# A third place for VectorE in the odd steps: seven subtractions of the row maxima per pair of steps, the fold of the sums in their first round, and the last output written in two halves

## The chip, the cores and the metric

The kernel runs on one core of one Trainium2 chip. The metric is the device time of the program in microseconds (us), the median of several runs. Besides these runs there is one profiled execution, and all rows below are of that one.

## The reference, cut to what matters

```python
def reference(X, Wq, Wk, Wv, Wpost, ffn_weight, ffn_bias):   # X: 4 x 1024 x 128 float32
    xn = layernorm(X)
    Q, K, V = (xn @ W for W in (Wq, Wk, Wv))                 # 16 heads of width 64
    raw = einsum('bshe,bthe->bsth', Q, K / 8)
    attn = softmax(raw, axis=2)
    A = gelu(einsum('bsth,bthe->bshe', attn, V))
    s = xn + A @ Wpost
    xq = mx_quantize(xn)      # blocks of 32: divided by the block's scale, rounded to a 6-bit grid, times the scale
    wq = mx_quantize(ffn_weight)
    g = silu(xq @ wq.T + ffn_bias)
    return X + s * g
```

## The kernel before, in words

The work is a sequence of 64 *steps* `s`. Two consecutive steps are one pair: the even one takes queries 0 to 511 of two heads of one batch, the odd one queries 512 to 1023 of the same heads. A step has four *rounds* `r`, and each round handles two tiles of 128 keys, `j = 2r` and `j = 2r + 1`. Every engine walks through the same double loop over `s` and `r` with its own instruction list, in program order, and semaphores join them.

TensorE's round has this order: `peak`, the raw scores of a *later* step (product of the rounded parts alone, two matmuls into the two banks of `peaks`), whose only purpose is the maximum of each row; `score` for tile 2r; `score` for tile 2r + 1; a second `peak`; then `weigh` for the two tiles of the round before, the product of probabilities and values into `acc`. Each `score` is three pairs of matmuls of split operands (L530), the two halves of the array working side by side, and a fourth pair (L537) that adds minus the row maxima out of `max_rows`. Where a next head has to be projected, the second `score` of a round is written mixed with that projection (L436), and the second peak's two matmuls are among it. Value projections (L448) and small transposes stand in some rounds too. `peaks` exists once: `peak_ready` lets no new peak start until VectorE has reduced the one before. `scores` exists twice: a tile may be written when the tile two before it has been read.

VectorE's round has the reduction of the first peak (`reduce_peaks`, L1066), then for the tiles listed in `BY_VECTOR` the subtraction of the maxima out of `scores` into `probs` (`subtract_maxima`, L1099), then the reduction of the second peak, and smaller work. For a tile that VectorE subtracts, TensorE leaves out the fourth pair. Before, these are tiles 0, 2, 4 and 6 in even steps and tile 0 in odd ones; the last step (63) follows the even list. `maxima` of the next step are joined and transposed in round 1 (`join_maxima`, `turn_squares`) and spread through DRAM into `max_rows` and `max_rep`. In the odd steps VectorE also quantises one tile of 128 rows for the gate: part 0 at the end of round 1, part 1 in round 2 just ahead of the second reduction, part 2 at the end of round 2, part 3 at the head of round 3 (`quantise_tile`, L1018 to L1029). Three odd steps, one ahead of each new batch, have one more operation there, `low_x` (L1052).

ScalarE takes the exponentials (L787), in the order that `order(s)` gives: in a round whose even tile goes to VectorE, the odd tile first. GpSimd (POOL) adds the eight probability tiles of a step into `prob_sum`, seven additions (L937), and multiplies the outputs of the step two before by the inverse sums (`normalise`, L893). `fold_sums` (L1104) on VectorE folds a finished `prob_sum` and waits for the seventh addition; `invert_sums` follows after a trip through DRAM. The fold of step s - 1 stands in round 3 of each step, in step 63 in round 1.

In step 0 no maxima are ahead yet: each round has three peaks, of which ScalarE copies the first into `att[0]` (`copy_peaks`), from where `reduce_copied` (L1059) reduces it. The start before that has eight first peaks, with `warm` matmuls between them (L605).

After step 63 TensorE runs `post` (L661), the output projection, chunk by chunk: eight chunks `c` of four tiles of 128 rows. Chunks 0 and 1 are run together head by head, then 2, 3 and so on. A chunk's bank of `scores` is used again two batches later: chunk 4 waits until chunk 0 has been read (`post_read`). VectorE's `result` adds xn (L1209), multiplies by the gate (L1212) and adds the input (L1215), and SyncE (SP) stores the chunk.

## Time and profile before

| | |
|---|---|
| median of 3 runs | 1353.72 us (1353.44 to 1354.28) |
| the profiled execution, its own time | 1353.71 us |
| its span | 1351.9 us |
| TensorE (PE) busy | 1332.1 us, 99% |
| GpSimd (POOL) busy | 1177.3 us, 87% |
| VectorE (DVE) busy | 1117.5 us, 83% |
| ScalarE (ACT) busy | 764.4 us, 57% |
| one pair of steps, 547.30 to 586.32 | 20.11 us + 18.91 us |
| chain that ended last | PE 91%, POOL 2%, DVE 2%, DMA 2%, ACT 1% |

The profiled execution's own time lies 1.8 us above its span: what lies ahead of the first and behind the last recorded event. The granted clock of TensorE is 1.00 (the level of 2.4 GHz) in nearly every stretch. A busy share is a mean over the span; a matmul's recorded duration overlaps the next one's, so the distance between starts is what a matmul costs. On VectorE too an instruction begins before the one ahead has ended: a reduction is recorded with 1.23 us, and the next instruction starts 1.14 us after it. Lines such as L516 are those of the kernel before.

### The profile page before, as it was taken

Reading aid. Unit: us, or ns where it says so; the run is one execution under the profiler, and the core shown is the slowest. Engines: PE = TensorE matmul, PEld = TensorE weight load, DVE = VectorE, ACT = ScalarE, POOL = GpSimd, SP = SyncE. Lnnn points to the kernel's source line nnn. Section 1 sums busy time; section 2 is a strip of 40 time slices with the busy share of each in tenths; the row PEclk is TensorE's granted clock in tenths of the full one; section 3 lists DMA queues with packets and bytes.
Section 4 is the critical chain, followed back from the end, with each engine's and each line's share of the span. In section 5 each row is a group of like instructions: output and inputs, shape, how many; then the busy total and the mean of one; then the engine's idle time right before and its main releaser. Section 6 shows DMA issues by size and latency. Waiting matters only on the chain.

```text
span 1351.9 us, 27029 instructions
## 1 busy us (share of the span) xinstructions
PE 1332.1 (99%) x10076; PEld 777.9 (58%) x10076; DVE 1117.5 (83%) x1509; ACT 764.4 (57%) x1072; POOL 1177.3 (87%) x551
## 2 busy tenths in 40 slices
PE   7999999999999999999999999999999999999998
PEld 4555555555555555555555555555555555555488
DVE  7689888888888888888888889888888888888623
ACT  4555665555556566555556566555555655555583
POOL 3689999998999999998999999999899999999940
PEclk9999999999999999999999999999999999999999
DMA  2011212211221212211122121212112111211484
GB/s 84 17 50 58 65 43 81 58 47 53 65 60 48 66 58 59 64 58 50 58 66 57 43 66 58 63 45 66 56 43 58 49 41 37 66 50 32 154 269 149
DMA packets 110636, 88.20 MB, mean 65 GB/s; under 512 B 70446, under 2 KB 84526, under 8 KB 110508
## 3 DMA queue, kind: packets, MB, share of 16 engines
q1 hardware_dynamic: 110508, 86.48, 21.6%
q8 instruction: 82, 1.34, 0.4%
q14 instruction: 46, 0.38, 0.1%
HBM read 70.19 MB, written 16.25 MB: 64 GB/s over the span
## 4 chain that ended last, share of the span: by engine, by line
PE 91%; POOL 2%; DVE 2%; DMA 2%; ACT 1%; issue 1%; SPq 0%; POOLq 0%; DVEq 0%
PE acc L588 33%; PE scores L530 24%; PE peaks L516 13%; PE extra L436 8%; PE scores L537 6%; PE extra L448 4%; POOL prob_sum L937 2%; PE scores L661 2%; PE extra L477 1%; DVE half_maxes L1066 1%; DMA sum_scratch<-group_sums 1%; ACT probs L787 1%; PE extra L484 0%; PE extra L459 0%; DMA probs<-att_scratch 0%
## 5 line engine op out<-in xcount | busy, mean ns | idle before, releaser
L937 POOL TENSOR_TENSOR prob_sum<-prob_sum,probs 128x1024 f32<-128x1024 f32 x384 | 917.5, 2389 | 79.8 <-ACT probs L787 34.5
L1066 DVE TENSOR_REDUCE half_maxes<-peaks 128x2 f32<-128x1024 f32 x500 | 612.2, 1224 | 150.1 <-PE peaks L516 143.9
L787 ACT ACTIVATE probs<-scores 128x1024 f32<-128x1024 f32 x353 | 355.4, 1025 | 473.4 <-PE scores L537 473.4
L588 PE MATMUL acc<-probs,vals 128*64 128x512 f32 x2048 | 492.5, 601 | 0.0
L516 PE MATMUL peaks<-k_hi,q_hi 64*128 64x512 f32 x1008 | 277.6, 451 | 6.5 <-DVE half_maxes L1066 4.7
L530 PE MATMUL scores<-q_hi,k_hi 64*128 64x512 f32 x1024 | 251.6, 393 | 1.1 <-DVE probs L1099 1.1
L530 PE MATMUL scores<-q_hi,k_lo 64*128 64x512 f32 x1024 | 250.0, 390 | 0.0
L530 PE MATMUL scores<-q_lo,k_hi 64*128 64x512 f32 x1024 | 249.0, 389 | 0.0
L588 PEld LDWEIGHTS acc<-probs,vals 128*64 128x64 f32 x2048 | 128.0, 136 | 210.1 <-issue 201.7
L516 PEld LDWEIGHTS peaks<-k_hi,q_hi 64*128 64x128 f32 x1008 | 116.6, 183 | 195.1 <-DVE half_maxes L1066 116.8
L1099 DVE TENSOR_TENSOR probs<-scores,max_rep 128x1024 f32<-128x1024 f32 x159 | 193.1, 1214 | 7.1 <-PE scores L530 5.7
L537 PE MATMUL scores<-max_rows,minus_r 64*128 64x512 f32 x690 | 182.1, 389 | 0.0
L937 POOL TENSOR_TENSOR prob_sum<-probs 128x1024 f32<-128x1024 f32 x64 | 153.6, 2399 | 23.7 <-ACT probs L787 23.7
L787 ACT ACTIVATE probs<-probs 128x1024 f32<-128x1024 f32 x159 | 170.0, 1069 | 1.9 <-DVE probs L1099 1.9
L530 PEld LDWEIGHTS scores<-q_lo,k_hi 64*128 64x128 f32 x1024 | 118.9, 185 | 22.0
L530 PEld LDWEIGHTS scores<-q_hi,k_lo 64*128 64x128 f32 x1024 | 118.9, 184 | 18.2
L530 PEld LDWEIGHTS scores<-q_hi,k_hi 64*128 64x128 f32 x1024 | 118.9, 185 | 15.8 <-issue 3.4
L893 POOL TENSOR_TENSOR att<-raw,inv_sum 128x512 f32<-128x512 f32 x64 | 98.2, 1534 | 20.5 <-DMA inv_sum<-inv_scratch 20.5
L537 PEld LDWEIGHTS scores<-max_rows,minus_r 64*128 64x128 f32 x690 | 86.8, 184 | 12.9
L1104 DVE TRANSPOSE_TENSOR_REDUCE group_sums<-prob_sum 128x32 f32<-128x1024 f32 x64 | 79.0, 1234 | 6.4 <-POOL prob_sum L937 6.4
L448 PEld LDWEIGHTS extra<-w_v,xTs 128*64 128x64 f32 x1024 | 57.3, 137 | 28.1 <-issue 27.0
L448 PE MATMUL extra<-w_v,xTs 128*64 128x128 f32 x1024 | 69.1, 276 | 0.2 <-DVE q_lo L1046 0.2
(170 smaller groups left out, 1223.7 us busy)
## 6 DMA issues: line engine op xcount, KB each, us to landing
max_rep<-max_scratch SPq DMA_DIRECT2D x63, 512.0 KB, 4.0
inv_sum<-inv_scratch SPq DMA_DIRECT2D x128, 128.0 KB, 2.9
att_scratch<-att SPq DMA_DIRECT2D x48, 256.0 KB, 2.3
probs<-att_scratch SPq DMA_DIRECT2D x8, 512.0 KB, 5.5
max_scratch<-turned SPq DMA_DIRECT2D x252, 1.0 KB
split_back<-att_scratch SPq DMA_DIRECT2D x6, 512.0 KB, 5.6
sums<-sum_scratch SPq DMA_DIRECT2D x128, 8.0 KB, 2.1
out_dram<-xn SPq DMA_DIRECT2D x8, 256.0 KB, 3.7
```

Source lines behind the costliest of these rows:

```text
L436: return mm(extra[:, :], left[own[h], at:at + P], right[own[h], halves[half]], start=(h == 0 and i == 0), stop=(h == 1 and i == 2), tile_p ...
L448: last = mm(w[own[h], t * P:(t + 1) * P], xT[:, tokens:tokens + DH], w_v[:, at:at + P], start=True, stop=True, tile_position=col[h])
L516: return mm(peaks[:, h, :], q_hi[z][own[h], t * P:(t + 1) * P], k_hi[z][own[h], keys], start=True, stop=True, tile_position=row[h])
L530: return mm(w[:, h, :], left[z][own[h], ks], right[z][own[h], qs], start=(i == 0), stop=(i == 2 and by_vector(s, j)), tile_position=row[h])
L537: return mm(w[:, h, :], sign[own[h], :], rows[own[h], :], start=False, stop=True, tile_position=row[h])
L588: last = mm(acc[own[h], :], vals[(s // 2) % 2][:, j, own[h]], probs[j][:, h, :], start=(k == 0), stop=(k == KT - 1), tile_position=col[h])
L787: sa.activation(probs[j][:, :, :], src[:, :, :], ACT.Exp, scale=DH ** -0.5).then_inc(probs_ready, 1)
L893: gp.tensor_tensor(by_32(att[p % HP][:, halves[s % 2]]), by_32(raw[s % 2][:, :]), inv[s % 2][:, :].rearrange("p (i b) -> p b i", i=SQ), AL ...
L937: gp.tensor_tensor(prob_sum[s % 2][:, :, :], before[:, :, :], probs[order(s)[j]][:, :, :], ALU.add).then_inc(probs_summed, 1)
L1066: v.tensor_reduce(half_maxes[:, :, f // 2, f % 2], peaks[:, :, :], AX.X, ALU.max).then_inc(peaks_read, 1)
L1099: v.tensor_tensor(probs[j][:, :, :], scores[j % 2][:, :, :], max_rep[s % 2][:, :, :], ALU.subtract).then_inc(subtracted, 1)
L1104: v.tensor_reduce(group_sums[:, :], prob_sum[s % 2][:, :, :].rearrange("p h (b i) -> p (h b) i", i=SQ), AX.X, ALU.add, apply_transpose=Tru ...
```

## The change

It has eight parts. (1) `BY_VECTOR` of the odd steps goes from tile 0 to tiles 0, 4 and 6. (2) The fold that stood in round 3 of the odd steps goes to their first round; in step 63 it goes from round 1 to round 0. (3) In step 0 the copied peak is reduced after the second peak rather than ahead of it. (4) `warm` has one matmul rather than two. (5) ScalarE runs one exponential on a spare value ahead of the first copies. (6) GpSimd gets, behind its last `normalise`, a multiplication and an addition for each of the eight chunks: rows xn times gate, plus the input. (7) `result` on VectorE has two operations in place of three, the product of the projection and the gate and one addition, and waits for GpSimd's. (8) The last chunk is projected, combined and stored in two halves, the second one through `acc`.

```diff
@@ -92,7 +92,7 @@
-    BY_VECTOR = ((0, 2, 4, 6), (0,))
+    BY_VECTOR = ((0, 2, 4, 6), (0, 4, 6))
     def by_vector(s, j):
         return s > 0 and j in BY_VECTOR[s % 2 if s < NS - 1 else 0]
...
@@ -180,6 +180,9 @@
         x_back = [rows_back[0][:, :], rows_back[1][:, :], k_lo_back[1][:, 0:HALF], k_lo_back[1][:, HALF:S], raw[0][:, :], inv[0][:, :], raw[1][:, :], inv[1][:, :]]
         TC = HALF // P
         NC = NT // TC
+
+        pieces = [(c, 0, TC) for c in range(NC - 1)] + [(NC - 1, 0, TC // 2), (NC - 1, TC // 2, TC // 2)]
+        lies_in = lambda c, t0: acc[:, :] if t0 > 0 else scores[c // 2 % 2][:, c % 2, :]
         scores = [ctx.enter_context(nc.psum_tensor(f"scores{u}", [P, 2, HALF], F32)) for u in (0, 1)]
         acc = ctx.enter_context(nc.psum_tensor("acc", [P, HALF], F32))
...
@@ -393,10 +396,10 @@
             sp.wait_ge(normalised, NS)
             for c in range(4, NC):
                 load_x_back(c)
-            for c in range(NC):
-                sp.wait_ge(result_done, c + 1)
-                sp.dma_start(out_t[:, c * TC:(c + 1) * TC, :], xn[c // 2][:, c % 2 * TC:(c % 2 + 1) * TC, :]).then_inc(written, 16)
-            sp.wait_ge(written, 16 * NC)
+            for i, (c, t0, nt) in enumerate(pieces):
+                sp.wait_ge(result_done, i + 1)
+                sp.dma_start(out_t[:, c * TC + t0:c * TC + t0 + nt, :], xn[c // 2][:, c % 2 * TC + t0:c % 2 * TC + t0 + nt, :]).then_inc(written, 16)
+            sp.wait_ge(written, 16 * len(pieces))
         @block.tensor
         def _(pe):
...
@@ -601,8 +604,7 @@
             def warm():
-                for _ in range(2):
-                    mm(acc[:, :], ones_r[:, :], max_rows[0][:, :], start=True, stop=True)
+                mm(acc[:, :], ones_r[:, :], max_rows[0][:, :], start=True, stop=True)
             pe.wait_ge(consts_set, N_SET)
...
@@ -653,13 +655,14 @@
             weigh(NS - 1, 6)
             weigh(NS - 1, 7)
-            def post(p, half):
+            def post(p, half, t0=0, nt=TC):
                 b, h = p // HP, p % HP
-                for t in range(TC):
+                w = lies_in(2 * b + half, t0)
+                for t in range(t0, t0 + nt):
                     for i in (0, 1):
                         tokens = half * HALF + t * P + i * DH
-                        last = mm(scores[b % 2][own[i], half, t * D:(t + 1) * D], home[p][:, tokens:tokens + DH], wp[:, h, :],
-                                  start=(h == 0 and t == 0), stop=(h == HP - 1 and t == TC - 1), tile_position=col[i])
+                        last = mm(w[own[i], (t - t0) * D:(t - t0 + 1) * D], home[p][:, tokens:tokens + DH], wp[:, h, :],
+                                  start=(h == 0 and t == t0), stop=(h == HP - 1 and t == t0 + nt - 1), tile_position=col[i])
                 if h == HP - 1:
                     last.then_inc(post_done, 1)
...
@@ -672,9 +675,12 @@
             for b in range(1, B):
                 for half in (0, 1):
                     above(pe, post_read, 2 * b + half - 3)
-                    for p in range(b * HP, (b + 1) * HP):
-                        pe.wait_ge(gelu_done, p + 1)
-                        post(p, half)
+                    if (b, half) == (B - 1, 1):
+                        pe.wait_ge(acc_read, NS)
+                    for t0, nt in [(t0, nt) for c, t0, nt in pieces if c == 2 * b + half]:
+                        for p in range(b * HP, (b + 1) * HP):
+                            pe.wait_ge(gelu_done, p + 1)
+                            post(p, half, t0, nt)
         @block.scalar
         def _(act):
...
@@ -793,6 +799,8 @@
             for p in (0, 1):
                 square(p)
                 root(p)
+
+            sa.activation(spare[:, :], eps[:, :], ACT.Exp)
             for half in (0, 1):
                 copy_xT(("x", 0, half))
                 for name in "qk":
...
@@ -940,6 +948,14 @@
             normalise(NS - 2)
             normalise(NS - 1)
+            for c in range(NC):
+                rows = xn[c // 2][:, c % 2 * TC:(c % 2 + 1) * TC, :]
+                pool.wait_ge(gated, c // 2 + 1)
+                gp.tensor_tensor(rows, rows, gate[:, c * TC:(c + 1) * TC, :], ALU.mult).then_inc(gated_rows, 1)
+                pool.wait_ge(gated_rows, c + 1)
+                pool.wait_ge(x_loaded_back[c], 16)
+                gp.tensor_tensor(rows, rows, x_back[c].rearrange("p (t d) -> p t d", d=D), ALU.add).then_inc(rest_ready, 1)
+
         @block.vector
         def _(dve):
             v = nc.vector
...
@@ -1146,9 +1162,7 @@
                     if half == 1 and r == 3:
                         quantise_tile(n, 3)
                     for at in todo[:1]:
-                        if s == 0:
-                            reduce_copied(r, *at)
-                        else:
+                        if s > 0:
                             reduce_peaks(*at)
                     if by_vector(s, 2 * r):
                         subtract_maxima(s, 2 * r)
...
@@ -1156,10 +1170,10 @@
                         gate_argument(n - 1)
                     if half == 1 and r == 2:
                         quantise_tile(n, 1)
-                    if half == 1 and r == 3 and s < NS - 1:
-                        fold_sums(s - 1)
                     for at in todo[1:2]:
                         reduce_peaks(*at)
+                    if s == 0:
+                        reduce_copied(r, *todo[0])
                     if r == (1 if s > 0 else 2) and s + 1 < NS:
                         join_maxima(s + 1)
                     if r == 1 and s > 1 and (half == 1 or False or s == NS - 2):
...
@@ -1181,7 +1195,7 @@
                         quantise_tile(n, 2 * r - 2)
                     if half == 1 and r == 2 and turns_x:
                         low_x(("x", later, 0))
-                    if s > 0 and half == 0 and r == 3 or s == NS - 1 and r == 1:
+                    if s > 0 and (half, r) in ((0, 3), (1, 0)):
                         fold_sums(s - 1)
                     if r == 3 and s == NS - 1:
                         invert_sums(NS - 2)
...
@@ -1201,26 +1215,23 @@
                         if half == 0 and r == 3 and n % HP == 5:
                             block_inverse(later)
-            def result(c):
+            def result(i):
+                c, t0, nt = pieces[i]
                 b, half = c // 2, c % 2
-                rows = xn[b][:, half * TC:(half + 1) * TC, :]
-                as_rows = lambda a: a.rearrange("p (t d) -> p t d", d=D)
-                dve.wait_ge(post_done, c + 1)
-                v.tensor_tensor(rows, as_rows(scores[b % 2][:, half, :]), rows, ALU.add).then_inc(post_read, 1)
-                dve.wait_ge(post_read, c + 1)
-                dve.wait_ge(gated, b + 1)
-                v.tensor_tensor(rows, rows, gate[:, c * TC:(c + 1) * TC, :], ALU.mult).then_inc(res_step, 1)
-                dve.wait_ge(res_step, c + 1)
-                dve.wait_ge(x_loaded_back[c], 16)
-                v.tensor_tensor(rows, rows, as_rows(x_back[c]), ALU.add).then_inc(result_done, 1)
+                ts = slice(half * TC + t0, half * TC + t0 + nt)
+                gates = gate[:, b * NB + half * TC + t0:b * NB + half * TC + t0 + nt, :]
+                dve.wait_ge(post_done, i + 1)
+                dve.wait_ge(gated_rows, c + 1)
+                v.tensor_tensor(gates, lies_in(c, t0)[:, 0:nt * D].rearrange("p (t d) -> p t d", d=D), gates, ALU.mult).then_inc(post_read, 1)
+                dve.wait_ge(post_read, i + 1)
+                dve.wait_ge(rest_ready, c + 1)
+                v.tensor_tensor(xn[b][:, ts, :], xn[b][:, ts, :], gates, ALU.add).then_inc(result_done, 1)
             gate_argument(NP - 1)
             fold_sums(NS - 1)
             invert_sums(NS - 1)
-            for c in (0, 1):
-                result(c)
-            for c in range(2, NC):
-                result(c)
+            for i in range(len(pieces)):
+                result(i)
 _INS = ["L0_attn_X", "L0_attn_Wq", "L0_attn_Wk", "L0_attn_Wv", "L0_attn_Wpost", "L0_ffn_weight", "L0_ffn_bias"]
```

The list of VectorE's instructions in an odd step, rounds 1 (its end) to 3. First the kernel before: the three L1018 to L1020 are part 0 of the quantisation, L1066 is the reduction of a peak, L1104 the fold.

```order
L1018 TENSOR_TENSOR extra<-extra,small 128x128
L1019 TENSOR_SCALAR quant_tmp<-extra 128x128
L1020 SCALAR_TENSOR_TENSOR extra<-quant_tmp,extra 128x128
L1066 TENSOR_REDUCE half_maxes<-peaks 128x2
L1022 SCALAR_TENSOR_TENSOR quant_tmp<-quant_tmp,extra 128x128
L1023 TENSOR_TENSOR extra<-extra,quant_tmp 128x128
L1024 TENSOR_TENSOR extra<-extra,quant_tmp 128x128
L1066 TENSOR_REDUCE half_maxes<-peaks 128x2
L1026 SCALAR_TENSOR_TENSOR extra<-extra,quant_tmp 128x128
L1027 SCALAR_TENSOR_TENSOR extra<-extra,quant_tmp 128x128
L1029 TENSOR_TENSOR quant<-extra,blk_max 128x128
L1066 TENSOR_REDUCE half_maxes<-peaks 128x2
```

The same stretch in the changed kernel, where L1082 is the reduction, L1115 the subtraction of the maxima, and L1034 to L1045 the quantisation.

```order
L1034 TENSOR_TENSOR extra<-extra,small 128x128
L1035 TENSOR_SCALAR quant_tmp<-extra 128x128
L1036 SCALAR_TENSOR_TENSOR extra<-quant_tmp,extra 128x128
L1082 TENSOR_REDUCE half_maxes<-peaks 128x2
L1115 TENSOR_TENSOR probs<-scores,max_rep 128x1024
L1038 SCALAR_TENSOR_TENSOR quant_tmp<-quant_tmp,extra 128x128
L1039 TENSOR_TENSOR extra<-extra,quant_tmp 128x128
L1040 TENSOR_TENSOR extra<-extra,quant_tmp 128x128
L1082 TENSOR_REDUCE half_maxes<-peaks 128x2
L1042 SCALAR_TENSOR_TENSOR extra<-extra,quant_tmp 128x128
L1043 SCALAR_TENSOR_TENSOR extra<-extra,quant_tmp 128x128
L1045 TENSOR_TENSOR quant<-extra,blk_max 128x128
```

Round 2 has a subtraction between its first reduction and part 1 of the quantisation, with the second reduction behind both. In round 3, which is not shown, the subtraction stands where the fold stood.

The other place on VectorE is the last step, 63, from its round 0 on. Before:

```order
L1099 TENSOR_TENSOR probs<-scores,max_rep 128x1024 x2
L1039 TENSOR_TENSOR gate<-extra,bias 128x128
L1110 TENSOR_REDUCE sums_flat<-sums 128x8
L1112 RECIPROCAL sums_flat<-sums_flat 128x8
L1018 TENSOR_TENSOR extra<-extra,small 128x128
L1019 TENSOR_SCALAR quant_tmp<-extra 128x128
L1020 SCALAR_TENSOR_TENSOR extra<-quant_tmp,extra 128x128
L1104 TENSOR_REDUCE group_sums<-prob_sum 128x32
L1099 TENSOR_TENSOR probs<-scores,max_rep 128x1024
```

And in the changed kernel, from the subtraction of round 0 of that step:

```order
L1115 TENSOR_TENSOR probs<-scores,max_rep 128x1024
L1120 TENSOR_REDUCE group_sums<-prob_sum 128x32
L1115 TENSOR_TENSOR probs<-scores,max_rep 128x1024
L1055 TENSOR_TENSOR gate<-extra,bias 128x128
L1126 TENSOR_REDUCE sums_flat<-sums 128x8
L1128 RECIPROCAL sums_flat<-sums_flat 128x8
```

The fold now stands between the subtractions of rounds 0 and 1. On GpSimd the end of the list before is

```order
L893 TENSOR_TENSOR att<-raw,inv_sum 128x512 x2
```

and in the changed kernel (the first three of the eight chunks)

```order
L901 TENSOR_TENSOR att<-raw,inv_sum 128x512 x2
L954 TENSOR_TENSOR xn<-xn,gate 128x512
L957 TENSOR_TENSOR xn<-xn,rows_back 128x512
L954 TENSOR_TENSOR xn<-xn,gate 128x512
L957 TENSOR_TENSOR xn<-xn,rows_back 128x512
L954 TENSOR_TENSOR xn<-xn,gate 128x512
L957 TENSOR_TENSOR xn<-xn,k_lo_back 128x512
```

So all sixteen row operations stand behind the last `normalise`.

## Rows read from the trace of the kernel before

**Rows 1.** Costliest groups of the page: busy and mean ns, then idle before and its releaser.
```profile
L1066 DVE TENSOR_REDUCE half_maxes<-peaks 128x2 f32<-128x1024 f32 x500 | 612.2, 1224 | 150.1 <-PE peaks L516 143.9
L1099 DVE TENSOR_TENSOR probs<-scores,max_rep 128x1024 f32<-128x1024 f32 x159 | 193.1, 1214 | 7.1 <-PE scores L530 5.7
```

**Rows 2.** Waits: engine, line, releaser, us in total, times, longest.
```profile
PEld peaks L516 <- DVE half_maxes L1066: 116.8, 159, 1.8
POOL prob_sum L937 <- ACT probs L787: 58.2, 63, 5.6
```

**Rows 3.** An odd step: length, busy PE, PEld, DVE, ACT, POOL, clock, DMA.
```profile
567.41:586.32 18.91, 18.91 (x130) 10.39 (x130) 15.74 (x25) 10.56 (x16) 18.19 (x10) 1.00 0.20 60
```

**Rows 4.** TensorE, timeline of rounds 2 and 3 of that odd step: start, duration.
```profile
577.39 0.39 PE L537 MATMUL scores<-max_rows,minus_r 64*128 64x512 f32 x2
577.62 0.40 PE L530 MATMUL scores<-q_hi,k_hi 64*128 64x512 f32 x2
...
578.64 0.50 PE L516 MATMUL peaks<-k_hi,q_hi 64*128 64x512 f32 x2
...
580.94 0.50 PE L516 MATMUL peaks<-k_hi,q_hi 64*128 64x512 f32 x2
...
583.10 0.39 PE L516 MATMUL peaks<-k_hi,q_hi 64*128 64x512 f32 x1
...
584.11 1.94 PE L588 MATMUL acc<-probs,vals 128*64 128x512 f32 x8
```

**Rows 5.** VectorE, timeline of the same odd step.
```profile
572.51 1.23 DVE L1066 TENSOR_REDUCE half_maxes<-peaks 128x2 f32<-128x1024 f32 x1 [1.07 <-PE peaks L516]
...
577.36 1.23 DVE L1066 TENSOR_REDUCE half_maxes<-peaks 128x2 f32<-128x1024 f32 x1
578.50 0.28 DVE L1022 SCALAR_TENSOR_TENSOR quant_tmp<-quant_tmp,extra 128x128 f32<-128x128 f32 x1
...
579.48 1.23 DVE L1066 TENSOR_REDUCE half_maxes<-peaks 128x2 f32<-128x1024 f32 x1
...
581.49 1.22 DVE L1066 TENSOR_REDUCE half_maxes<-peaks 128x2 f32<-128x1024 f32 x1
```

**Rows 6.** GpSimd, timeline: the last three additions of the even step ahead.
```profile
563.42 7.43 POOL L937 TENSOR_TENSOR prob_sum<-prob_sum,probs 128x1024 f32<-128x1024 f32 x3
```

**Rows 7.** VectorE and TensorE in an odd step with `low_x`.
```profile
305.30 0.69 DVE L1052 TENSOR_TENSOR xT_lo<-xTs,xT_hi 128x512 fp32r<-128x512 f32 x1
...
307.38 0.50 PE L516 MATMUL peaks<-k_hi,q_hi 64*128 64x512 f32 x1
```

**Rows 8.** TensorE: a warm pair, and a mixed peak of step 0.
```profile
23.41 0.73 PE L605 MATMUL acc<-max_rows,ones_r 128*128 128x512 f32 x2
...
37.01 0.50 PE L516 MATMUL peaks<-k_hi,q_hi 64*128 64x512 f32 x1 [0.69 <-DVE half_maxes L1066]
```

**Rows 9.** Last step: VectorE's subtraction of round 0 and its fold, TensorE's score of tile 6.
```profile
1272.11 1.22 DVE L1099 TENSOR_TENSOR probs<-scores,max_rep 128x1024 f32<-128x1024 f32 x1 [1.41 <-DMA max_rep<-max_scratch]
...
1281.30 1.25 DVE L1104 TRANSPOSE_TENSOR_REDUCE group_sums<-prob_sum 128x32 f32<-128x1024 f32 x1 [0.48 <-POOL prob_sum L937]
...
1283.71 0.51 PE L530 MATMUL scores<-q_hi,k_hi 64*128 64x512 f32 x2 [1.13 <-DVE probs L1099]
```

**Rows 10.** The end: GpSimd's last operation, TensorE at chunk 4 and its last, VectorE's last.
```profile
1320.76 1.53 POOL L893 TENSOR_TENSOR att<-raw,inv_sum 128x512 f32<-128x512 f32 x1 [18.88 <-DMA inv_sum<-inv_scratch]
...
1318.25 6.31 PE L661 MATMUL scores<-w_v,probs 128*64 128x128 f32 x112
1325.04 8.08 PE L661 MATMUL scores<-w_v,probs 128*64 128x128 f32 x144 [0.47 <-ACT probs L732]
1332.95 14.14 PE L661 MATMUL scores<-w_v,att 128*64 128x128 f32 x256
...
1348.59 0.69 DVE L1215 TENSOR_TENSOR xn<-xn,inv_sum 128x512 f32<-128x512 f32 x1
```

**Rows 11.** GpSimd: four additions of the step of rows 7.
```profile
297.93 10.32 POOL L937 TENSOR_TENSOR prob_sum<-prob_sum,probs 128x1024 f32<-128x1024 f32 x4
```

2 lines of the change are left out of this document (1 added, 1 removed).

## The prediction

> **What bounds the kernel now.** I read the page first: TensorE is busy 99% of the span, VectorE 83%, GpSimd 87%, and the chain that ended last is 91% TensorE. So work taken off TensorE counts, as long as TensorE doesn't wait for someone instead. Then the waits: the largest that TensorE has are those of the peaks for VectorE's reduction, 159 of them [rows 2]. Most are hidden, since weights wait there while earlier matmuls still run. But they say where the two engines touch: one set of `peaks`, and each new peak needs the last one reduced. Last I read the timeline of an odd step round by round. Its 18.91 us hold 15.74 us of VectorE's work [rows 3], 3.2 us of slack, and the question is in which round the slack lies.
>
> **Subtractions in rounds 2 and 3 of the odd steps.** TensorE gains one pair of matmuls a tile. Starts of neighbouring pairs lie 0.23 us apart [rows 4]. 31 odd steps (1 to 61) with two more tiles make 31 x 2 x 0.23 = 14.3 us, if it can run ahead. VectorE pays 1.21 us a subtraction [rows 1]; like a reduction it overlaps the next instruction a little, so it moves what follows by 1.13.
>
> Round 2, in the step of the rows. The first reduction starts at 577.36 and ends at 578.59. The second peak starts at 578.64 [rows 4, 5], right behind it: TensorE already waits here (tile 5 starts at 577.62, and its four pairs are done at 577.62 + 4 x 0.23 = 578.54), so the 0.23 that round 2 saves ahead of this peak is lost. Now VectorE subtracts from 578.50 on, then does part 1 of the quantisation, which before ran from 578.50 to 579.48, and the second reduction starts at 579.48 + 1.13 = 580.61 and ends at 581.84. Before it ended at 580.71, and the first peak of round 3 started at 580.94, when the products were done [rows 4, 5]. Now that peak waits until 581.89: 0.95 later. Round 3 saves its 0.23 and loses 0.08 again: its first reduction also moves by 1.13, from 581.49 to 582.62, ends at 583.85, and the peak in the mixed part, at 583.10 before, would be ready at 583.10 + 0.95 - 0.23 = 583.82. Net **0.80 us later in each odd step** at the products that started at 584.11 [rows 4, 5]. The second reduction of round 3 finds its peak late rather than the reverse, and the even step's first peak waits for nothing, so the shift neither grows nor is won back: even rounds are TensorE's own.
>
> The three steps with `low_x` have that operation of 0.69 on VectorE ahead of round 3, and their mixed peak, at 307.38, already waited for its reduction [rows 7]; it moves with it by the whole 1.13. For steps 1 to 59: 27 x 0.80 + 3 x 1.13 = **25.0 us**. Step 61 I leave out: GpSimd's additions after it run without a wait for ScalarE to the end, so they set the end and not TensorE.
>
> **The fold in round 0 of the odd steps.** It leaves round 3 where a subtraction takes its place (nothing gained), and enters a gap of 1.07 us ahead of the reduction at 572.51 [rows 5]. It needs 1.15, so 0.0 to 0.1. It waits for GpSimd's seventh addition, which ends at 570.85 [rows 6], 0.6 us before VectorE is free at 571.44. Cover gone, each us of lateness beyond about 0.4 would delay the second peak of round 1.
>
> **Last step.** Here the same line puts the fold ahead of the subtraction of tile 2. GpSimd's addition comes at 1281.3, whereas VectorE is free for the fold after the subtraction of tile 0, at 1272.11 + 1.13 = 1273.2 [rows 9]: it stands still for 8 us. Behind the fold are queued the subtraction of tile 2, the quantisation and tile 4; TensorE's score of tile 4 waits for tile 2, that of tile 6 for tile 4. Before, tile 6 started at 1283.71, already late by 1.13 for a fold [rows 9]. Now tile 4 starts there and tile 6 one round later, some 4 us. The output projection starts that much later.
>
> **The end.** GpSimd's sixteen row operations stand behind the last `normalise`, from 1320.76 to 1322.29 after a wait of 18.88 for a DMA [rows 10]. Chunk 0's gated rows come one operation later. I have no row of that form: half of an addition of twice the size makes 1.24 [rows 6], the `normalise` of the same size took 1.53 [rows 10]; I take 1.4, nearer to the second for its equal size. 1322.3 + 1.4, VectorE's read of 0.7 and 0.1 between them: chunk 4 can start at 1324.5 rather than 1318.25 [rows 10]. The 4 us of the last step lie in this wait and don't add. From the start of chunk 4 to the end at 1347.09 TensorE took 28.84, of which 0.47 was a wait for ScalarE that the delay covers: 28.37. So the projection ends at 1352.9. Then VectorE needs two operations of half a chunk, about 0.42 each, between half of the 0.69 of a whole one and all of it, and ends near 1353.8, against 1348.59 + 0.69 = 1349.28. The last store is half as large: before 2.6 until the span's end, now between 2.0 and 2.6. Together **+4.3**, bounds +1 (if the sums come home earlier) and +7.
>
> What GpSimd does afterwards matters less: sixteen operations at 1.3 to 1.63 with their gaps end between 1343 and 1348.4. But while `low_x` ran, which reads two SBUF tensors, four additions took 10.32 us [rows 7, 11] where three take 7.43 [rows 6], so about 9.9: 0.4 lost beside one VectorE instruction of 0.69. Seven additions of VectorE at the end read two SBUF tensors as well; at 0.4 to 0.69 each GpSimd ends at 1346 to 1353, still ahead of the last half.
>
> The Trainium skill, "SBUF — State Buffer", section "Who interferes with whom", says that a VectorE instruction with two SBUF inputs contends with a GpSimd instruction that reads SBUF, and that the loser blocks fully. By that rule the end could be GpSimd's, up to 0.5 us later than I sum. The same section lets an instruction with one SBUF input alone, which would leave the new subtractions harmless to GpSimd.
>
> **The start.** `warm` loses one of two matmuls of 0.33 (0.73 recorded for the pair with overlap) [rows 8], four times, between peaks that then go at VectorE's own pace of 1.14: -1.3. In step 0 the peak in the mixed part waited 0.69 for the reduction at 35.74, which stood behind that of the copy [rows 8]. Reduced first it starts about 0.5 earlier, in four rounds: -2.0. The table load of the exponential falls into time when ScalarE waits for TensorE, before and after: 0. Bounds of the start -1 and -4.
>
> **Sum**: 25.0 + 4.3 - 3.3 = +26.0. The profiled execution took 1353.71 and the median is 1353.72, so I forecast **1379.7 us**, slower by 1.9%. The odd steps can be off by a third: 17 to 31.
>
> **Rivals.** (a) Faster: VectorE keeps up. Its share only rises from 83% to 88%, and if the second reduction of round 2 came in time, by quantisation work that is shorter or an overlap that the rows don't show, all 14.3 would be kept: 1353.7 - 14.3 - 3.3 + 4.3 = **1340.4**. It decides at the slack ahead of round 3's first peak: 0.23 us (580.94 less 580.71), against 1.13 added. That speaks against it. (b) No change: the saved pairs pay for about all of the stall, and what is left is start and end: 1353.7 + 1.0 = **1354.7**. (c) Much slower: the fold in round 0 waits for GpSimd in every pair, late by an addition (2.5): after the gap of 0.6 and slack of 0.4 that is 1.5 in 31 steps, 1379.7 + 46 = **1426**. Against it: GpSimd waits for ScalarE once per pair, 63 times in all [rows 2], so it starts each even step fresh, and longer pairs give it more time. (d) The last line doesn't do what it says: the early fold is early in every odd step but 63, where it waits. I have put this into the forecast; if it were harmless the end would not move, for GpSimd's chain hides it.
>
> **How the numbers follow.** A measurement of this kernel tells 0.2% from no change, 2.7 us. My forecast has 0.80, (a) 0.12, (b) 0.03, (c) 0.05. The range comes from the forecast's own bounds: low 17 + 1 - 4 = +14 gives 1368, which I widen to 1365 for a mis-sized stall; high 31 + 7 - 1 = +37 gives 1390. The other cases, 0.20, are outside. Faster 0.12, same 0.03, slower 0.85.
>
> **What would show it.** In the changed profile the first peak of round 3 in odd steps should start right behind the second reduction of round 2, some 0.95 us after the products end; the pair should last about 39.8 rather than 39.0; VectorE's idle time before the reduction of round 1 should vanish; the wait of peaks for reductions should grow by some 25 us; the fold of step 63 should stand in front of a late tile 2; the projection of chunk 4 should wait for VectorE some 2 us. Wrong it is if pairs get shorter than 39.0.

## The result, and the profile after

The changed kernel takes **1397.01 us** (median of 4 runs, 1394.79 to 1397.89) against 1353.58 beside it (1352.64 to 1354.28): ratio 1.031, interval 1.030 to 1.033. That is 43.4 us slower; the forecast was 26. The profiled execution took 1397.02, its span 1395.2 (1351.9 before), so the two traces differ by the whole of it: 43.3. TensorE runs 128 matmuls fewer (9948 for 10076) and yet is busy 1334.7 us for 1332.1, some of them at the low clock, as shown below; it is idle 60.5 us for 19.8. It has less work and waits more.

The place is found with one instruction that stands once in every step from step 2 on: the reduction of the row sums (L1110 before, L1126 after). Its start after less its start before is called the *offset* of the step below. The differences of the offsets, read from its 64 rows:

| stretch | us | forecast |
|---|---|---|
| start and step 1 (read in step 2) | -0.27 | -2.5 |
| 27 ordinary pairs, to step 62 | +23.65, 0.88 each | +20.8, 0.80 each and none for step 61 |
| 3 pairs with `low_x` | +5.14, +5.28, +4.33 = 14.75 | +3.4 |
| behind step 62: step 63, projection, store | +5.2 | +4.3 |
| sum | +43.3 | +26.0 |

The ordinary pairs and the end went about as forecast. The three pairs with `low_x` did not: 11.4 us of the missing 17.3 are theirs.

**An ordinary pair.** The first reduction of the even step comes at 522.11 and 561.94: 39.83, forecast 39.8. VectorE in the odd step, timeline (start, us, instruction, idle before):

```profile
544.79 1.22 DVE L1082 TENSOR_REDUCE half_maxes<-peaks 128x2 f32<-128x1024 f32 x1
545.92 1.24 DVE L1120 TRANSPOSE_TENSOR_REDUCE group_sums<-prob_sum 128x32 f32<-128x1024 f32 x1
547.09 1.23 DVE L1082 TENSOR_REDUCE half_maxes<-peaks 128x2 f32<-128x1024 f32 x1
...
551.88 1.23 DVE L1082 TENSOR_REDUCE half_maxes<-peaks 128x2 f32<-128x1024 f32 x1
553.02 1.21 DVE L1115 TENSOR_TENSOR probs<-scores,max_rep 128x1024 f32<-128x1024 f32 x1
554.15 0.28 DVE L1038 SCALAR_TENSOR_TENSOR quant_tmp<-quant_tmp,extra 128x128 f32<-128x128 f32 x1
...
555.13 1.23 DVE L1082 TENSOR_REDUCE half_maxes<-peaks 128x2 f32<-128x1024 f32 x1
```

and TensorE beside it:

```profile
553.16 0.49 PE L519 MATMUL peaks<-k_hi,q_hi 64*128 64x512 f32 x2
553.59 1.94 PE L591 MATMUL acc<-probs,vals 128*64 128x512 f32 x8
556.41 0.50 PE L519 MATMUL peaks<-k_hi,q_hi 64*128 64x512 f32 x2 [0.89 <-DVE half_maxes L1082]
```

Each item that the forecast asked for is there: the fold (545.92) fills the idle 1.07 of [rows 5] with nothing late behind it; the subtraction (553.02) and part 1 of the quantisation stand ahead of the second reduction of round 2; that ends at 556.36 and the first peak of round 3 starts at 556.41, after 0.89 of idle time. Over the whole run, by the waits (total, times, longest):

```profile
PEld peaks L519 <- DVE half_maxes L1082: 152.8, 160, 1.8
...
PE peaks L519 <- DVE half_maxes L1082: 34.8, 60, 1.4
PE extra L439 <- DVE quant L1045: 6.7, 3, 2.2
```

In [rows 2] the weights waited 116.8; they now wait 36 longer, where some 25 were forecast. The matmuls themselves waited 4.7 for the reductions before; now 34.8. The last row is new: three waits, one in each `low_x` step.

**A step with `low_x`.** Timeline of VectorE at the end of round 2:

```profile
310.23 0.30 DVE L1043 SCALAR_TENSOR_TENSOR extra<-extra,quant_tmp 128x128 f32<-128x128 f32 x1
310.57 2.59 DVE L1068 TENSOR_TENSOR xT_lo<-xTs,xT_hi 128x512 fp32r<-128x512 f32 x1
313.08 0.28 DVE L1045 TENSOR_TENSOR quant<-extra,blk_max 128x128 f32<-128x128 f32 x1
```

GpSimd at the same time:

```profile
307.74 4.87 POOL L945 TENSOR_TENSOR prob_sum<-prob_sum,probs 128x1024 f32<-128x1024 f32 x2 [0.76 <-ACT probs L793]
312.57 1.98 POOL L901 TENSOR_TENSOR att<-raw,inv_sum 128x512 f32<-128x512 f32 x1
```

TensorE, which ends the wait at 313.46:

```profile
310.05 0.50 PE L519 MATMUL peaks<-k_hi,q_hi 64*128 64x512 f32 x2 [0.88 <-DVE half_maxes L1082]
...
313.46 0.76 PE L439 MATMUL extra<-xT_hi,wq_hi 64*128 64x512 f32 x1 [2.22 <-DVE quant L1045]
...
317.18 2.98 PE L591 MATMUL acc<-probs,vals 128*64 128x512 f32 x8
```

The stretches around it (length, busy us of PE, PEld, DVE, ACT, POOL, then the granted clock, DMA share, GB/s):

```profile
308.00:313.00 5.00, 2.36 (x14) 0.81 (x10) 4.83 (x7) 1.13 (x2) 4.86 (x3) 0.95 0.36 114
313.00:320.00 7.00, 6.54 (x26) 3.60 (x27) 4.45 (x6) 2.46 (x3) 3.59 (x2) 0.55 0.15 42
320.00:325.00 5.00, 5.00 (x48) 3.56 (x46) 3.28 (x3) 1.76 (x3) 2.72 (x2) 1.00 0.00 0
```

The same subtraction of 0.69 in [rows 7] is recorded with 2.59 here. It was issued within GpSimd's second addition (some 310.2 to 312.6, half of the 4.87 each) and is recorded until 0.55 us behind that addition's end; I read this as standing still until about that end and then working for its 0.69, and an experiment below tests it. Quantisation's last instruction stands behind it; the mixed projection writes `extra`, which that instruction has to read first, and TensorE waits 2.22. After that wait the granted clock is 0.55, near the level of 1.2 GHz, until about 320: the products take 2.98, in an ordinary round 1.94.

**Start and end.** TensorE's first block of transposes and the first projections, after (the clock between 10 and 17 us is 0.76, as a mean):

```profile
10.05 1.09 PE L462 MATMUL scores<-ident,xn 128*64 128x128 f32 x16 [1.97 <-DVE xn L990]
11.91 1.80 PE L429 MATMUL acc<-xTs,att 128*64 128x512 f32 x4 [0.77 <-ACT xTs L743]
13.43 1.99 PE L429 MATMUL extra<-xTs,att 128*64 128x512 f32 x4
```

The end on TensorE (it answers to [rows 9, 10]):

```profile
1321.33 0.79 PE L533 MATMUL scores<-q_hi,k_hi 64*128 64x512 f32 x2 [4.33 <-DVE probs L1115]
...
1363.94 14.19 PE L664 MATMUL scores<-w_v,probs 128*64 128x128 f32 x256 [1.91 <-DVE gate L1225]
```

GpSimd, the last `normalise` and the first row operation:

```profile
1360.34 1.53 POOL L901 TENSOR_TENSOR att<-raw,inv_sum 128x512 f32<-128x512 f32 x1 [18.29 <-DMA inv_sum<-inv_scratch]
1361.82 1.27 POOL L954 TENSOR_TENSOR xn<-xn,gate 128x512 f32<-128x512 f32 x1
```

The late fold stalls the last step by 4.33, as forecast, and chunk 4 waits only 1.91 since the 4 us have gone into the same wait. It starts 7.6 after its place in the kernel before, moved by the loop's 38.1 (1318.25 + 38.1 = 1356.4); forecast 6.25.

### The profile page after: what moved, and what is told of

Read it like the earlier page. It is cut to its first block, busy times and chain, and to the rows that moved or that the text cites. A ratio compares the mean times of both kernels' runs of the same rounds, so it can differ in the third digit from the quotient of the medians.

```text
span 1395.2 us, 26858 instructions
## 1 busy us (share of the span) xinstructions
PE 1334.7 (96%) x9948; PEld 774.6 (56%) x9948; DVE 1192.7 (85%) x1565; ACT 766.2 (55%) x1073; POOL 1199.7 (86%) x567
## 4 chain that ended last, share of the span: by engine, by line
PE 84%; DVE 10%; issue 3%; ACT 2%; POOL 1%; DMA 0%; SPq 0%; POOLq 0%; DVEq 0%
PE acc L591 28%; PE scores L533 24%; PE peaks L519 12%; PE extra L439 7%; PE scores L540 4%; PE extra L451 4%; DVE half_maxes L1082 4%; DVE probs L1115 3%; PE scores L664 2%; POOL prob_sum L945 1%; PE extra L480 1%; DVE extra L1040 1%; DVE extra L1039 1%; PE extra L487 0%; DVE quant_tmp L1038 0%
## 5 line engine op out<-in xcount | busy, mean ns | idle before, releaser
L1082 DVE TENSOR_REDUCE half_maxes<-peaks 128x2 f32<-128x1024 f32 x500 | 612.0, 1224 | 116.7 <-PE peaks L519 110.5
L793 ACT ACTIVATE probs<-scores 128x1024 f32<-128x1024 f32 x291 | 294.9, 1024 | 507.0 <-PE scores L540 507.0
L519 PE MATMUL peaks<-k_hi,q_hi 64*128 64x512 f32 x1008 | 281.5, 455 | 37.2 <-DVE half_maxes L1082 34.8
L1115 DVE TENSOR_TENSOR probs<-scores,max_rep 128x1024 f32<-128x1024 f32 x221 | 268.5, 1215 | 5.3 <-PE scores L533 3.9
L793 ACT ACTIVATE probs<-probs 128x1024 f32<-128x1024 f32 x221 | 235.9, 1068 | 11.1 <-DVE probs L1115 11.0
L540 PE MATMUL scores<-max_rows,minus_r 64*128 64x512 f32 x566 | 158.8, 392 | 0.0
L540 PEld LDWEIGHTS scores<-max_rows,minus_r 64*128 64x128 f32 x566 | 76.0, 186 | 9.9
```

Of the source, the lines that this page charges most:

```text
L519: return mm(peaks[:, h, :], q_hi[z][own[h], t * P:(t + 1) * P], k_hi[z][own[h], keys], start=True, stop=True, tile_position=row[h])
L540: return mm(w[:, h, :], sign[own[h], :], rows[own[h], :], start=False, stop=True, tile_position=row[h])
L793: sa.activation(probs[j][:, :, :], src[:, :, :], ACT.Exp, scale=DH ** -0.5).then_inc(probs_ready, 1)
L1082: v.tensor_reduce(half_maxes[:, :, f // 2, f % 2], peaks[:, :, :], AX.X, ALU.max).then_inc(peaks_read, 1)
L1115: v.tensor_tensor(probs[j][:, :, :], scores[j % 2][:, :, :], max_rep[s % 2][:, :, :], ALU.subtract).then_inc(subtracted, 1)
```

## The experiments

Ratios are to the kernel before on the same chip (1354.2 to 1354.9). Offsets are of the profiled execution.

### Which tile, and which part of the change

```diff
 a1_one_tile    (changed kernel)  BY_VECTOR = ((0, 2, 4, 6), (0,))
 a3_tile_6      (changed kernel)  BY_VECTOR = ((0, 2, 4, 6), (0, 6))
 a4_tile_4      (changed kernel)  BY_VECTOR = ((0, 2, 4, 6), (0, 4))
 a2_loop_alone  (kernel before)   BY_VECTOR = ((0, 2, 4, 6), (0, 4, 6)), fold in round 0 of odd steps, 63 as before
```

This block and the ones with names of kernels further down tell the edits in short; they are not cuts of the code.

> The changed kernel with the odd steps' list back at tile 0 alone; the fold in round 0, the start and the end stay changed. Round theory (VectorE's round 2 is too long, so the first peak of round 3 waits): pairs are back at 39.0 us, the three steps with low_x lose nothing, and what is left is the start (-1.1 in the profile after) and the end (+5.2): 1353.6 + 4.1 = 1357.7 us. Fold theory (the fold in round 0 costs the 0.87 per pair): pairs stay near 39.8 us, about 1357.7 + 27 = 1385 us.

> The kernel before with nothing but the list (0, 4, 6) and the fold in round 0 of the odd steps, step 63 as before. If the loop holds the loss: 28 pairs by 0.87 and three with low_x by 4.9 make +39, 1392.6 us. If start or end feed back into the pairs, it comes out elsewhere.

> The changed kernel with tiles 0 and 6 in the odd steps. Round theory: round 2 is as before, round 3 has a subtraction where it had a fold, so nothing stalls and each pair is 0.23 us shorter: 1357.7 - 31 x 0.23 = 1350.6 us. Tile theory (each subtraction costs VectorE's 1.13 us of its total load, wherever it stands): half of the loss stays, about 1357.7 + 19 = 1377 us.

> The changed kernel with tiles 0 and 4 in the odd steps. Round theory: the wait of round 2 is there in full and round 3 saves no pair of matmuls, so 0.95 to 1.0 us a pair and the whole loss in the three steps with low_x: 1357.7 + 28 x 0.95 + 3 x 4.9 = 1399 us, at most some us below or above the changed kernel's 1397. Tile theory: half of the loss, about 1377 us.

| kernel | median us | ratio, interval | offset at step 62 |
|---|---|---|---|
| tile 0 | 1360.16 | 1.0038, 1.0023 to 1.0053 | -2.9 |
| loop alone | 1393.64 | 1.029, 1.027 to 1.030 | +40.1 |
| tiles 0, 6 | 1354.18 | 0.9992, 0.9983 to 1.0002 | -6.5 |
| tiles 0, 4 | 1398.45 | 1.032, 1.031 to 1.034 | +34.6 |

The loop alone and tiles 0, 4 came as forecast (1392.6, 1399). Tile 0 alone and tiles 0, 6 came 2.5 and 3.6 us later than I had summed, and the end is where. One tile decides. Tile 4, whose subtraction stands in round 2 ahead of the second reduction, makes all of the loss; tile 6 in round 3 gains 0.2 us a pair. VectorE has the same added work in both. With tile 0 alone the fold in the first round costs nothing: the offset stays between -2.9 and -2.5 from step 2 to 62. The old end on the slow loop adds nothing behind step 62 (span +40.1 in all). The new end costs much more where it isn't covered: in the kernel with tiles 0 and 6 the span is 2.7 longer than before, from -6.5 at step 62, so 9.2.

### What bounds round 2

```diff
+                elif part == 1 and src is None:
+                    pass
                 elif part == 1:
```

This kernel leaves out part 1 of the quantisation of the row tiles (L1038 to L1040), so its gate, and with it its output, has other values; the counts that wait for it are adapted (not shown).

> The changed kernel without the three instructions of part 1 of the row tiles' quantisation, 0.98 us of VectorE in round 2 of the odd steps between the exponential's argument and the second reduction. Round theory (the 0.87 us a pair are what VectorE's queue in round 2 takes beyond TensorE's round, and the low_x pairs have the port block on top): the peak of round 3 waits no longer, all pairs fall back to 38.95 us or a little under (38.8 as with tiles 0 and 6): 27 x 0.87 to 1.1 us = 24 to 30 us less, 1367 to 1373, with the low_x pairs still some 2 to 4 us over the others each. Rival (the stall is not made by VectorE's queue but by the maxima's way through the DMA or by TensorE's order): 1395 to 1397. Third (the low_x pairs' excess needs VectorE late as well): they lose 4 us each on top, 1357 to 1360.

The median of its ten runs is 1358.89 us. Eight of them took 1355.74 to 1359.96; two took 1840.13 and 4247.44, for a reason that nothing here shows, and are left out of the ratio, 1.0024 (1.0013 to 1.0035). Both new subtractions are in place. Round 2 has 0.98 us less and the pairs are 0.10 us *shorter* than before. So the 0.87 of a pair are VectorE's queue in this round. The theory's number (1367 to 1373) was missed since the `low_x` pairs fell too, to +0.6 each: there the subtraction was issued at 302.79, nearer to the end of GpSimd's addition, and took 1.11. The third case, 1357 to 1360, is what came. VectorE's row, and GpSimd's beside it:

```profile
302.79 1.11 DVE L1070 TENSOR_TENSOR xT_lo<-xTs,xT_hi 128x512 fp32r<-128x512 f32 x1
```

```profile
300.96 5.18 POOL L945 TENSOR_TENSOR prob_sum<-prob_sum,probs 128x1024 f32<-128x1024 f32 x2 [0.76 <-ACT probs L793]
```

### The three pairs with `low_x`

```diff
+                    if half == 1 and r == 2 and turns_x:
+                        low_x(("x", later, 0))
                     if half == 1 and r in (1, 2):
                         quantise_tile(n, 2 * r - 2)
-                    if half == 1 and r == 2 and turns_x:
-                        low_x(("x", later, 0))
```

> The changed kernel, with the subtraction of low_x issued ahead of the second part of the quantisation (in the rounds 2 that have both, three pairs) and not behind it. In the changed kernel these three pairs are 5.1, 5.3 and 4.3 us longer than before instead of 0.87 (offsets of the row-sum reduction from step to step), and their subtraction lasts 2.59 us instead of 0.69 and ends with the GpSimd addition beside it. Port theory (a VectorE instruction with two inputs from SBUF stands still until GpSimd's instruction has ended; the quantisation's end, behind it in VectorE's queue, is late, TensorE waits 2.2 us for it and then runs at the low clock): issued some 1.5 us earlier, the subtraction falls at the end of the GpSimd instruction before or in the gap between two, so it lasts 0.7 to 1.2 us and the quantisation comes last, undelayed; TensorE's wait of 2.2 us goes and the clock stays up. 3 x (2.5 to 4) us = 8 to 12 us less: 1385 to 1389. Rival (the order does not matter, the three pairs are long because VectorE has 0.69 us more work in a round that it bounds, and the clock falls by itself): 1395 to 1397. Second rival (it meets the full GpSimd instruction instead of half of it): the subtraction lasts up to 2.9 us, 1397 to 1400.

1387.91 us (1384.1 to 1390.84), ratio 1.0253 (1.0235 to 1.0272). The pairs are +1.20, +1.17 and +1.23 where they were +5.14, +5.28, +4.33. The six instructions of this line by tile (min/median/max ns), in the kernel before:

```profile
L1052 DVE TENSOR_TENSOR xT_lo<-xTs,xT_hi x6: 639/666/693, 305.3 to 948.8; 128x512 fp32r<-128x512 f32 x6
```

in the changed kernel:

```profile
L1068 DVE TENSOR_TENSOR xT_lo<-xTs,xT_hi x6: 641/1617/2622, 310.6 to 980.0; 128x512 fp32r<-128x512 f32 x6
```

and here:

```profile
L1068 DVE TENSOR_TENSOR xT_lo<-xTs,xT_hi x6: 640/696/774, 309.0 to 968.1; 128x512 fp32r<-128x512 f32 x6
```

The Trainium skill, "SBUF — State Buffer", section "Who interferes with whom", says that a VectorE instruction with two SBUF inputs and a GpSimd instruction that reads SBUF contend, and that the loser is blocked fully. These rows agree: 1.9 us above its own 0.69, up to GpSimd's next boundary. Here it is issued 2.16 us behind the start of GpSimd's two additions rather than 2.83, close to the boundary between them, and takes 0.75. VectorE in that stretch:

```profile
308.95 0.75 DVE L1068 TENSOR_TENSOR xT_lo<-xTs,xT_hi 128x512 fp32r<-128x512 f32 x1
...
310.28 0.29 DVE L1045 TENSOR_TENSOR quant<-extra,blk_max 128x128 f32<-128x128 f32 x1
```

GpSimd beside it:

```profile
306.79 5.15 POOL L945 TENSOR_TENSOR prob_sum<-prob_sum,probs 128x1024 f32<-128x1024 f32 x2 [0.78 <-ACT probs L793]
```

Three kernels now have it in three places, counted from the start of the two additions: issued at 1.83 (without part 1), 2.16 (here) and 2.83 (changed kernel), it ends at 2.94, 2.91 and 5.42. Less its own 0.69 that is 2.25, 2.22 and 4.73, each time 0.1 to 0.4 ahead of the end of an addition (half of 5.18 or 5.15, and all of 4.87). The subtractions of the maxima read one input from PSUM and only one from SBUF; all 221 of them in the changed kernel took 1.19 to 1.23, whatever GpSimd did.

TensorE beside it:

```profile
309.09 0.51 PE L519 MATMUL peaks<-k_hi,q_hi 64*128 64x512 f32 x2 [0.89 <-DVE half_maxes L1082]
310.67 0.47 PE L439 MATMUL extra<-xT_hi,wq_hi 64*128 64x512 f32 x1 [0.39 <-issue]
...
312.88 1.94 PE L591 MATMUL acc<-probs,vals 128*64 128x512 f32 x8
```

and its stretch, with the clock at 1.00:

```profile
311.00:318.00 7.00, 6.77 (x56) 4.30 (x54) 5.15 (x6) 3.04 (x4) 6.43 (x4) 1.00 0.15 42
```

With these rows the excess of a step is split. From the peak to the mixed projection 3.41 us in the changed kernel (310.05 to 313.46), 1.58 here (309.09 to 310.67): 1.8 of waiting. From there to the products 3.72 (to 317.18) against 2.21 (to 312.88), and the products with what follows 0.7 longer (317.18 to 320.00, 312.88 to 315.04): 2.2 of low clock. Together 4.0, and 5.14 - 1.20 = 3.9. More than half of the price of this wait was the clock behind it.

The kernel with tiles 0 and 4 shows the same without the exchange. Its subtraction of `low_x` is blocked as long (2.62, 2.62 and 2.64) and TensorE waits 2.02, 2.01 and 2.02, but the clock falls behind the second wait only. Its three pairs are +3.05, +4.04 and +3.08. The first of them:

```profile
312.31 0.47 PE L439 MATMUL extra<-xT_hi,wq_hi 64*128 64x512 f32 x1 [2.02 <-DVE quant L1045]
```

```profile
312.00:319.00 7.00, 6.47 (x52) 4.16 (x54) 4.01 (x6) 2.09 (x3) 6.09 (x3) 1.00 0.14 40
```

That kernel has no subtraction in round 3, so the comparison with +5.14 isn't clean; within it, the low clock goes with one microsecond. Why the clock falls behind one wait of 2.0 and not behind another isn't shown.

### The end

```diff
 b2_last_fold:   if s > 0 and (half, r) in ((0, 3), (1, 1 if s == NS - 1 else 0)):
 b4_rows_early:  GpSimd: normalise(NS - 1) behind the rows of chunks 0 and 1, not ahead of them
```

> The changed kernel, with the fold of the sums of the last step back in its round 1. In the changed kernel the fold (issued at 1318.92) waits 7.50 us for GpSimd's sum with the second exponential argument behind it, and TensorE's first product of tile 4 waits 4.33 us for that. Theory 1 (the stall is real but the end hangs on GpSimd's last rows, which wait for the DMA of the row sums, and this chain starts at GpSimd's sum and not at TensorE): the products of the last step end about 4 us earlier, the projections too, and chunk 4's wait for VectorE grows from 1.9 to about 6; time 1395 to 1398, no change. Theory 2 (TensorE's chain is the end): 1392.5 to 1393.5, 4 us less.

> The changed kernel, with GpSimd's multiplication and addition of the first two chunks issued ahead of the last normalisation instead of behind it. In the changed kernel the last normalisation waits 18.3 us for the row sums (to 1360.3), the first product of rows and gate comes behind it at 1361.8, VectorE's first result at 1363.2 and chunk 4's projection waits for that (1.9 us, up to 4.3 us in the kernel with tiles 0 and 4). Theory: it waits no longer, and what it would wait for next is its own data: 1.9 us less, and no more, so 1394 to 1396; the last results are not late (GpSimd is done 10 us before the end). Rival (GpSimd and VectorE share their time in the chunks and this is what sets the end): 1397. Second rival (TensorE had lost its clock in the wait): up to 3.5 us less, 1393.5.

The fold back in its place: 1396.18 (1394.85 to 1397.75), no difference to the changed kernel; TensorE reached the projection at 1327.44, not 1333.86 (0.8 of the difference is a shorter loop in this profile), and chunk 4 then waited:

```profile
1363.26 15.59 PE L664 MATMUL scores<-w_v,probs 128*64 128x128 f32 x256 [6.99 <-DVE gate L1225]
```

The rows of chunks 0 and 1 early: 1392.86 (1391.94 to 1394.79), and chunk 4 waits for nothing:

```profile
1361.73 14.17 PE L664 MATMUL scores<-w_v,probs 128*64 128x128 f32 x256
```

The span is 2.2 shorter for a wait of 1.91, as expected; the median lies 4 us lower, under my 1394, and the trace doesn't show the rest. Behind step 62 the end now costs 2.4 us (span +41.1, offset at step 62 +38.7) rather than 5.2. So about half of the 5.2 hung on GpSimd's row work behind the last `normalise`; the rest stays with the late fold, whose stall of 4.29 stands in this kernel too. Chunk 4 still starts 4.8 late (1361.73 for 1318.25 + 38.7), and what follows it is 2.4 us shorter than before.

### The start, and a kernel that beats both

```diff
 c1_start_alone        (kernel before)  start of the changed kernel
 c2_start_tile_6_fold  (the same)       + tiles 0 and 6, + fold in round 0 of odd steps but 63; old end
 c3_start_tile_6       (the same)       + tiles 0 and 6, fold as before
 c4_tile_6_new_end     (changed kernel) tiles 0 and 6, fold of 63 in round 1, rows of chunks 0 and 1 early
```

> The kernel before with the changed start alone: one warming matmul of two, the early Exp of ScalarE, the copied first reduction of step 0 behind the other work of its round. Spans go by the profiled execution. Theory (the start gains what was forecast, about 3 us, when TensorE's clock stays up through the first projections, and loses most of it where the clock falls there): the profile has the projections at about 11.9 either at 1.08 us, with step 1 2.8 us earlier than before, or at 1.6 to 1.8 us, with step 1 0.2 to 1.3 us earlier; single times fall in two groups about 2 us apart, and the median is 1351 to 1353. Rival (the start gains 3.3 always, as forecast, and the differences seen are of the loop): 1350.5 to 1351. Rival (no gain at all): 1354.

> The kernel before with the changed start, tiles 0 and 6 on VectorE in the odd step (not tile 4), the fold moved to round 1 of the odd step (its first, 0 in the code) but not in the last step, and the end as before. Theory (tile 6 gains 0.2 us a pair, as the kernel with tiles 0 and 6 showed: 5.3 us over 27 pairs; the end of the changed kernel is what cost that kernel 9 us behind step 62): 1354.3 - 5.3 - 1 to 3 (start) = 1346 to 1348, faster than before. Rival (the loop's 5.3 us are lost again in the old end, since the last row sums are late whatever came before): 1351 to 1353.

> As the run before (changed start, tiles 0 and 6, old end), but with the fold kept in round 4 of the odd step (3 in the code). It tells whether the fold had to move. VectorE has 1.21 us more in round 4 and lies 0.38 and 0.30 us idle before its next two reductions in the kernel before; theory: what does not fit into them, 0.5 us, stalls every pair: 28 x 0.5 = 14 us over the run before, 1358 to 1363. Rival (TensorE's own round is longer with a mixed peak and covers it): the same as the run before, 1346 to 1348.

> The changed kernel with tiles 0 and 6 (not 4), the fold of the last step back in its round 2 (1 in the code), and GpSimd's rows of chunks 0 and 1 ahead of the last normalisation. Theory (the kernel with tiles 0 and 6 alone lost 9 us behind step 62, 4 by the fold's stall and 4 to 5 by chunk 4's wait and the clock behind it; both go, and the halved last output ends 1.7 us sooner behind TensorE's last matmul, 3.1 us instead of 4.8): 1344 to 1346.5, and 1 to 2 us under the kernel with the old end. Rival (something else of the new end is late, such as GpSimd's rows for chunk 2 on behind the last normalisation): 1349 to 1352.

| kernel | median us | ratio, interval | offset at steps 2, 62 |
|---|---|---|---|
| start alone | 1351.52 | 0.9978, 0.9969 to 0.9986 | -2.9, -3.0 |
| tiles 0, 6, fold moved, old end | 1345.81 | 0.9938, 0.9925 to 0.9952 | -2.3, -7.5 |
| tiles 0, 6, fold as before | 1359.79 | 1.0038, 1.0025 to 1.0051 | -2.7, +4.5 |
| tiles 0, 6, mended new end | 1345.74 | 0.9933, 0.9919 to 0.9946 | -1.4, -7.6 |

The last two and the first came within their ranges, the second 0.2 us below its own; that the new end gains 1 to 2 us over the old one did not come. The start is worth 2.7 us; its times don't fall in two groups as I expected (1349.82 to 1352.51, spread evenly). **Tile 6 as the one added tile, with the fold moved and the changed start, beats both kernels: 8.4 us under the one before, 2.7 of them by the start.** With the fold left in round 3 it is 14 us slower than that, 8.3 over the start alone. VectorE's rows there:

```profile
582.33 1.21 DVE L1100 TENSOR_TENSOR probs<-scores,max_rep 128x1024 f32<-128x1024 f32 x1
583.46 1.23 DVE L1105 TRANSPOSE_TENSOR_REDUCE group_sums<-prob_sum 128x32 f32<-128x1024 f32 x1
584.62 1.19 DVE L1067 TENSOR_REDUCE half_maxes<-peaks 128x2 f32<-128x1024 f32 x1
```

Subtraction and fold stand both between the reductions of round 3 (the first at 581.19), where [rows 5] had the fold alone; the second reduction is late, and the pair grows by 0.2 (0.7 with `low_x`). The mended new end gains nothing over the old one that can be measured. In its profile TensorE waits for ScalarE four times in the projection behind its first chunks, 2.96 us in all, two of them here; with the old end it is once, 0.25. That these waits use up the gain is likely, but no run tests it.

```profile
1304.54 1.09 PE L664 MATMUL scores<-w_v,k_hi_back 128*64 128x128 f32 x16 [1.10 <-ACT k_hi_back L738]
...
1319.62 1.09 PE L664 MATMUL scores<-w_v,probs 128*64 128x128 f32 x16 [1.08 <-ACT probs L738]
```

## Why the prediction was wrong, point by point

- *Subtractions in rounds 2 and 3, 0.80 each odd step.* Right: 0.87, the peak behind the second reduction as written, 0.89 of idle time for my 0.95. The 0.07 over 26 pairs are 2 us. The kernels with one tile showed that the sum of both rounds is as told: round 2 loses, round 3 gains 0.2.
- ***The three steps with `low_x`, "it moves with it by the whole 1.13": the step that failed.*** It measured 4.9 (5.14, 5.28, 4.33), 11.4 us of the 17.3 that were missing. I took the subtraction's duration of 0.69 from [rows 7] as its own and moved it as a block. It was short there because it stood at a boundary of GpSimd's additions: at 305.30, 4.86 us into three that start at 300.44 and take 7.82 together. Put into one, it stood still for 1.9; a wait of TensorE followed, and the low clock. I had quoted the rule on two SBUF inputs for the end alone, where it changed little. With the block taken away the step cost 1.20, the 1.13 of the sum.
- *Step 61 left out.* Wrong by 0.9: its pair grew like the others. "GpSimd sets the end" was right for chunk 4, but GpSimd's own work is late with the loop.
- *The fold in round 0: 0.0 to 0.1.* Right: with tile 0 alone it cost nothing in a pair; rival (c) didn't come.
- *Last step and end, +4.3.* Mechanism right, 5.2: the fold stalls 4.33 and is hidden in chunk 4's wait. The chunk started 7.6 late, not 6.25, although GpSimd's first row operation took 1.27 for my 1.4: the last `normalise` itself came 1.5 us late against the loop (1360.34 for 1320.76 + 38.1). The stretch behind it was 0.4 shorter than summed.
- *The start, -3.3.* At the full clock it is 2.9 (start alone, tile 0 alone). In the changed kernel start and step 1 came to -0.27 rather than -2.5. Kernels with the same loop and the full clock in the first projections (`low_x` first, fold of 63 back) have -1.3 there, so 1.0 goes with the low clock of the changed kernel's profile. Another 0.7 belongs to step 1, in the kernels with the new start, tile 6 and the fold moved; its cause stays open.
- *Rivals (a) and (b).* (a) turned on the second reduction of round 2 coming in time. The kernel without part 1 made it so and lost the stall, yet not 14.3 us came back but 0.10 a pair, 3 in all. What TensorE gains by a left-out pair of matmuls is mostly spent at the next peak, which waits for VectorE anyway.
- *The range.* Its upper end, +37, let the odd steps be off by a third. An instruction that is blocked for most of its neighbour's duration isn't a third off: it took 2.59 for 0.69, and its step cost four times the 1.13.

## To carry to other kernels

Price an added instruction by the round in which it stands and by what waits behind it there: the same 1.21 us gained 5.3 us in round 3, where the fold had made room, and cost 36.5 in round 2 (from step 2 to step 62), in an engine with the same load. When an edit shifts an engine that shares SBUF with another, list every instruction that reads two SBUF inputs and see where in the neighbour's work it will fall; its duration in the old trace holds for its old place only. And faults in two parts of a change can hide in one wait: the fold back in its place paid nothing by itself, the rows early 4 us by themselves, and both together 8.4 (1354.18 to 1345.74, in the kernel with tiles 0 and 6). So a part that seems to cost nothing is tried again once its neighbour is mended.

## What the runs showed of the hardware that I had not expected

- The low clock behind a short wait can cost more than the wait: 2.2 us after 1.8 in the first `low_x` step. At the end it costs less than the wait, but still shows: where chunk 4 waited 4.2 us (tile 0 alone) or 6.99 (fold back) its 256 matmuls took 15.86 and 15.59, where it waited 1.91 or not at all 14.19 and 14.17.
- At the start, with the same code and idle TensorE before the first transposes, the clock was full or low from kernel to kernel. Of the fourteen profiles of this case, in four the idle time was 1.81 to 1.97 us and the projection at 11.9 took 1.57 to 1.80; in ten it was 0.77 to 1.68 and took 1.08:

```profile
9.96 1.09 PE L462 MATMUL scores<-ident,xn 128*64 128x128 f32 x16 [0.81 <-DVE xn L990]
11.82 1.08 PE L429 MATMUL acc<-xTs,att 128*64 128x512 f32 x4 [0.77 <-ACT xTs L743]
```

  These two rows are of the kernel with tile 0 alone. The idle time differs because the first warming block took 5.7 to 6.9 us with the same 18 matmuls. What made it differ stays open, and no run varied it alone. What makes the clock fall there isn't shown either; the two only went together.
- VectorE's last additions (two SBUF inputs) are blocked by GpSimd's row work too: 1.63 to 1.68 us beside it and 0.69 after it, in the kernel with tiles 0 and 6. Its multiplications of the same size, which read one input from PSUM, take 0.68 to 0.69 in both places.

```profile
1338.31 1.63 DVE L1228 TENSOR_TENSOR xn<-xn,gate 128x512 f32<-128x512 f32 x1
1344.57 0.69 DVE L1225 TENSOR_TENSOR gate<-scores,gate 128x512 f32<-128x512 f32 x1 [4.63 <-PE scores L664]
1345.29 0.69 DVE L1228 TENSOR_TENSOR xn<-xn,gate 128x512 f32<-128x512 f32 x1
```

  GpSimd loses in turn: its operation behind the one that blocked takes 1.6 to 1.7 where it takes 1.27 alone.
